# A two-block kernel (bidirectional Mamba, then a mixture of experts): the routed experts' outputs are scaled by ScalarE on their way out of PSUM and added up by GpSimd, in place of VectorE

## The chip, the cores and the metric

The program runs on one core of a Trainium2 chip. The metric is the time of one execution on the device, in microseconds (us). Engines are named as in the profile: PE is TensorE (PEld its weight loads), DVE is VectorE, ACT is ScalarE, POOL is GpSimd, SP is SyncE, which issues the transfers.

## The reference, cut to what matters

There are 16 sequences of 512 tokens with 128 channels. Each goes through a normalisation, a Mamba block run forwards and backwards (256 inner channels, 16 states), a second normalisation, and a mixture of eight routed experts, of which a token uses two, plus one shared expert:

```
gate_out = x @ gate_w
top_v, top_i = jax.lax.top_k(gate_out, TOP_K)            # TOP_K = 2 of 8
w = softmax over the chosen two, 0 elsewhere
swiglu(x, w1, w2, w3) = h * sigmoid(h) * (x @ w2) @ w3,  h = x @ w1
out = sum over e of swiglu(x, ew1[e], ew2[e], ew3[e]) * w[..., e]
out = out + swiglu(x, sw1, sw2, sw3)
```

All is float32. Every expert is computed for every token, and the weight `w` is zero where the token did not choose it. The change touches only the sum over experts.

## The kernel before, in words

All engines run programs written out by hand, in the same order of work: `passes` calls `body(b, ...)` for b = 0 to 16. Body b holds the scan of sequence b (both directions) beside the mixture of experts of sequence b-1, the preparation of the backward direction of b, and that of the forward direction of b+1. Body 0 has no experts, body 15 prepares nothing for a next sequence, body 16 has only the experts of sequence 15 (below: the tail). Bodies 1 to 14 are alike.

A body has 32 **slots**, one for each scan step: slots 0 to 15 are the 16 states forwards, 16 to 31 backwards. Within a slot s:

- DVE scans two halves of 128x512 (L792, reads `psA` in PSUM and `bt`), then multiplies each by `cb` into `g` (L802). Between the two L802 it makes `pf` (L891) from ScalarE's `tf` and the expert's first product in PSUM bank F0. After them it does its side work: `zs` or `u` (L832), `yg` (L850, shown as `acc`), statistics (L808), and in some slots the expert sum (L905).
- ACT first evicts an expert's two products as `tf` and `gf` (L686, L689: `expert_turns`), then writes the two `exp` tiles that the next slot's scans need (L604: `exps`, each waits for the `g` of the same half), then its side work: `xn`/`z` (L657), `th` (L622, L625), `ab`/`xb` (L641 to L645), and in slots 9 and 28 `ln1p` (L652, L653), which loads another activation table, computes, and loads the old one again.
- POOL first makes `bt` for the next slot (L430), then side work (`dt` L474, `v` L479, `hx`, `wg`, the output `fx` and `osb` L484, L487 in slot 0), then `act` (L520) from `pf` and `gf`.
- PE adds the previous slot's `g` into `psY` (L996), then its expert work and preparation: the down projection of an expert into PSUM bank F2 (L1122), convolutions (L1012), `skip_and_turn` (L1033, L1035), and last the two up projections into F0 and F1 (L1083, L1086).

The down projection of expert e takes two slots (`down_at`: part 0 and part 1). For e = 1 to 8 the part 1 slots are 15, 17, 19, 21, 24, 26, 28 and 30. Expert 0 is the shared one; ACT copies it to `facc` (L707). There is one bank F2, so PE waits at part 0 of expert e until that of e-1 has been read; before, that is a wait on `facc_s`. `expert_sum` does four instructions on DVE for each routed expert, one for each 128 tokens: `facc = F2 * wts + facc`, with the weight as a per-partition operand, in the part 1 slot. GpSimd's `output` reads `facc` at the end. Every wait is a semaphore count; an engine runs its own list strictly in order.

Of the kernel before, what the change touches and what calls it, by code (L numbers as in the profile page):

```python
# [70 lines left out]
def adaln_mamba_moe(nc, t, out):  # L71
# [3 lines left out]
    with ctx:  # L75
# [6 lines left out]
        def sem(name):  # L82
            return ctx.enter_context(nc.semaphore(name))
# [105 lines left out]
        pf = sb("pf", [P, 2, T])  # L189
        act = sb("act", [P, 3, 2, T])  # L190
        facc = sb("facc", [P, NT, D])
        osb = sb("osb", [P, NT, D])
# [67 lines left out]
        pf_s = sem("pf_s")  # L260
        act_s = sem("act_s")
        facc_s = sem("facc_s")
        gw_s = sem("gw_s")
# [143 lines left out]
        def _(pool):  # L407
# [73 lines left out]
            def output(fb):  # L481

                pool.wait_ge(facc_s, NX * NT * fb + NX * NT)
                g.tensor_tensor(fx[:, :, :], facc[:, :, :], over_tiles(modF[:, :]), ALU.mult).then_inc(o_s, 1)  # L484
                pool.wait_ge(o_s, 2 * fb + 1)
                wait(pool, out_d, 16 * fb)
                g.tensor_tensor(osb[:, :, :], fx[:, :, :], x2[:, :, :], ALU.add).then_inc(o_s, 1)  # L487

            def expert_weights(fb):
# [9 lines left out]
                pool.wait_ge(wts_s, q + 2)  # L499
                wait(pool, facc_s, NX * NT * fb)  # L500
                g.tensor_tensor(wts[:, :, :], hotw[:, 0, :, :], hotw[:, 1, :, :], ALU.add).then_inc(wts_s, 1)

            def ffn_side(fb, slot):
# [10 lines left out]
                if k is not None:  # L514
# [5 lines left out]
                    g.tensor_tensor(act[:, k // 2 % 3, k % 2, :], pf[:, k % 2, :], gf[:, k % 3, :], ALU.mult)\  # L520
                        .then_inc(act_s, 1)

            def gated_weights(b):
# [26 lines left out]
            def body(b, scan, ffn, last):  # L550
                for slot in range(STEPS):
# [12 lines left out]
                    if ffn:  # L564
                        ffn_side(b - 1, slot)

            passes(pool, body)
# [4 lines left out]
        def _(act_e):  # L572
# [118 lines left out]
            def ffn_side(fb, slot):  # L691
# [12 lines left out]
                if down_at(slot) == (0, 1):  # L704
                    act_e.wait_ge(F2_full, (DOWN + NE) * fb + DOWN + 1)
                    wait(act_e, o_s, 2 * fb)
                    s.activation(facc[:, :, :], F2[:, :], ACT.Copy).then_inc(F2_free, 1)  # L707

            for slot in range(STEPS):
# [38 lines left out]
        def _(dve):  # L748
# [144 lines left out]

            def expert_sum(fb, slot):

                down = down_at(slot)
                if down and down[0] and down[1]:
                    e = down[0]
                    dve.wait_ge(F2_full, (DOWN + NE) * fb + DOWN + e + 1)
                    if e == 1:  # L900
                        dve.wait_ge(F2_free, (DOWN + 1) * fb + DOWN + 1)
                        dve.wait_ge(wts_s, 3 * fb + 3)
                    wait(dve, facc_s, NX * NT * fb + NT * (e - 1))
                    for i in range(NT):
                        w.scalar_tensor_tensor(facc[:, i, :], F2[:, i * D:i * D + D],  # L905
                                               wts[:, i, ORDER[e]:ORDER[e] + 1], facc[:, i, :],
                                               ALU.mult, ALU.add).then_inc(facc_s, 1)

            def ffn_side(fb, slot):
# [28 lines left out]
            def body(b, scan_, ffn, last):  # L938
                for slot in range(STEPS):
# [10 lines left out]
                    if ffn:  # L950
                        ffn_side(b - 1, slot)
                        expert_sum(b - 1, slot)
                    if scan_ and slot - POST_F_SLOT in (0, 1):
# [6 lines left out]
        def _(pe):  # L960
# [95 lines left out]
            def ffn_side(fb, slot):  # L1056
                free = (DOWN + 1) * fb
                if slot - POSTB_SLOT in (0, 1):
                    half = slot - POSTB_SLOT
                    if half == 0:  # L1060
                        pe.wait_ge(acc_s, 4 * fb + 4)
                        wait(pe, facc_s, NX * NT * fb)
                    else:
# [25 lines left out]
            def ffn_late(fb, slot):  # L1089
# [22 lines left out]
                if down:  # L1112
                    e, part = down
                    if part == 0:
# [3 lines left out]
                        else:  # L1118
                            pe.wait_ge(facc_s, NX * NT * fb + NT * (e - 1))
                    for i in (2 * part, 2 * part + 1):  # L1120
# [57 lines left out]
```

## Time and profile before

| | |
|---|---|
| median of 3 runs | 2525.33 us (2525.15 to 2533.57) |
| the profiled execution | 2529.96 us |
| its span | 2528.1 us |
| busy in the span | DVE 91%, PE 82%, POOL 77%, ACT 60% |
| bodies 1 to 14 | 149.0 us each |
| body 15 | 144 us |
| body 16, the tail | 86 us |

The profiled execution lies 4.6 us over the median, 0.2%. Busy shares are means over the whole span. Since each engine works through its own list in order, the place to read is a slot: which engine had to wait in it, and for whom. The list of instructions in order of time shows that: its columns are the start (us from the span's start), how long, the engine, the line, the operation with its output and inputs, how many were merged into the row, and in brackets how long the engine had been idle before and who released it. Successive instructions of an engine overlap a little, so a row's duration is more than the distance to the next one's start.

### The profile page before, as it was taken

What the parts mean: (1) busy time and instruction counts of PE and PEld (TensorE: products, weight loads), DVE (VectorE), ACT (ScalarE), POOL (GpSimd) and SP (SyncE); (2) the same over time, 40 slices, a digit from 0 to 9 for tenths busy, and PEclk for the clock granted to TensorE, in tenths of its full rate; (3) what the DMA queues carried; (4) which work ended last, traced back from release to release, by engine and by line L of the source; (5) the groups of instructions that cost most, each with busy time, mean ns of one, the idle gap of its engine ahead of it and who ended that gap; (6) DMA issues with size and microseconds to landing.
All of it is one profiled execution on the core that took longest, in us unless ns stands there. A gap on an engine that the chain in (4) does not pass through costs nothing. (4 is left out here: it accounts for less than half of the span.)

```text
span 2528.1 us, 31606 instructions
## 1 busy us (share of the span) xinstructions
PE 2078.9 (82%) x9893; PEld 1307.9 (52%) x9893; DVE 2298.2 (91%) x3843; ACT 1505.8 (60%) x2468; POOL 1936.1 (77%) x1259
## 2 busy tenths in 40 slices
PE   3667887989888797988879888888988878898868
PEld 1344554545555465555546555454655545565545
DVE  1699999999999999999999999999999999999963
ACT  2545656665666666556666665666666576666633
POOL 1576888878788787878878788787878888787844
PEclk9678999989999998999999899898999999899989
DMA  3334243333433333342333333333333433333310
GB/s 85 127 126 143 100 131 119 110 131 109 137 105 125 122 111 131 110 139 101 118 131 110 131 109 131 118 110 125 118 131 109 137 112 111 132 112 130 109 55 5
DMA packets 112107, 291.16 MB, mean 115 GB/s; under 512 B 18260, under 2 KB 44724, under 8 KB 111940
## 3 DMA queue, kind: packets, MB, share of 16 engines
q1 hardware_dynamic: 111940, 289.15, 33.6%
q8 instruction: 78, 1.28, 0.2%
q14 instruction: 89, 0.73, 0.1%
HBM read 282.77 MB, written 6.34 MB: 114 GB/s over the span
## 5 line engine op out<-in xcount | busy, mean ns | idle before, releaser
L430 POOL TENSOR_TENSOR bt<-v,bb 128x1024 f32<-128x1024 f32 x512 | 1208.6, 2361 | 175.2 <-DVE psA L792 173.2
L792 DVE TENSOR_TENSOR_SCAN psA<-psA,bt 128x512 f32<-128x512 f32 x1024 | 1196.2, 1214 | 62.6 <-ACT psA L604 60.6
L604 ACT ACTIVATE psA<-dt,aneg 128x512 f32<-128x512 f32 x1024 | 687.8, 688 | 732.3 <-DVE g L802 731.8
L996 PEld LDWEIGHTS psY<-ident,g 128*128 128x128 f32 x4096 | 504.1, 149 | 428.1 <-DVE g L802 212.2
L996 PE MATMUL psY<-ident,g 128*128 128x128 f32 x4096 | 601.5, 290 | 129.2 <-DVE g L802 128.0
L802 DVE TENSOR_TENSOR g<-psA,cb 128x512 f32<-128x512 f32 x1024 | 673.4, 677 | 0.0
L520 POOL TENSOR_TENSOR act<-pf,gf 128x512 f32<-128x512 f32 x288 | 366.2, 1271 | 290.8 <-DVE pf L891 269.1
L1083 PE MATMUL F<-h2T,w 128*128 128x512 f32 x576 | 329.5, 656 | 100.4 <-DVE pf L891 99.5
L1122 PE MATMUL F<-w,act 128*128 128x128 f32 x2304 | 308.8, 277 | 14.5 <-DVE facc L905 8.3
L1086 PE MATMUL F<-h2T,w 128*128 128x512 f32 x576 | 314.0, 629 | 0.0
L1122 PEld LDWEIGHTS F<-w,act 128*128 128x128 f32 x2304 | 282.3, 193 | 29.5 <-POOL act L520 25.5
L1012 PE MATMUL psP<-xnT,wcT 128*128 128x512 f32 x512 | 255.2, 623 | 4.4 <-DVE u L832 2.1
L891 DVE SCALAR_TENSOR_TENSOR pf<-tf,F 128x512 f32<-128x512 f32 x288 | 195.0, 677 | 51.0 <-ACT tf L686 48.3
L686 ACT ACTIVATE tf<-F 128x512 f32<-128x512 f32 x288 | 170.2, 591 | 75.3 <-PE F L1083 74.9
L1083 PEld LDWEIGHTS F<-h2T,w 128*128 128x128 f32 x576 | 95.1, 197 | 212.1 <-DVE pf L891 163.7
L689 ACT ACTIVATE gf<-F 128x512 f32<-128x512 f32 x288 | 172.7, 600 | 51.6 <-PE F L1086 51.0
L1028 PE MATMUL psP<-xnT,wzT 128*128 128x512 f32 x128 | 96.0, 842 | 123.0 <-DVE zs L832 121.7
L1086 PEld LDWEIGHTS F<-h2T,w 128*128 128x128 f32 x576 | 115.8, 201 | 150.1 <-issue 149.5
L905 DVE SCALAR_TENSOR_TENSOR facc<-F,wts,facc 128x128 f32<-128x128 f32 x512 | 143.3, 343 | 5.2 <-PE F L1122 5.2
L1012 PEld LDWEIGHTS psP<-xnT,wcT 128*128 128x128 f32 x512 | 92.8, 202 | 76.7 <-issue 67.6
L625 ACT ACTIVATE th<-psP 128x512 f32<-128x512 f32 x128 | 75.7, 592 | 52.9 <-PE psP L1028 50.8
L474 POOL TENSOR_TENSOR dt<-xb,ab 128x1024 f32<-128x1024 f32 x32 | 75.3, 2355 | 33.9 <-ACT ab L652 33.8
(130 smaller groups left out, 1700.1 us busy)
## 6 DMA issues: line engine op xcount, KB each, us to landing
bb<-bc_rows SPq DMA_DIRECT2D x256, 512.0 KB, 3.7
cb<-bc_rows SPq DMA_DIRECT2D x256, 512.0 KB, 3.7
x<-in_L_attn_x SPq DMA_DIRECT2D x16, 256.0 KB, 4.3
out_x<-osb SPq DMA_DIRECT2D x16, 256.0 KB, 4.5
modA<-mod_table SPq DMA_DIRECT2D x16, 192.0 KB, 4.4
w<-in_L_ffn_ew SPq DMA_DIRECT2D x2, 1024.0 KB
bc_rows<-xd SPq DMA_DIRECT2D x32, 64.0 KB, 3.2
modG<-mod_table SPq DMA_DIRECT2D x16, 64.0 KB, 4.0
```

The costliest lines, as they stand in the source:

```text
L430: g.tensor_tensor(bt[:, n % 2, :, :], v[d][:, :, :], bb[:, n // 2 % 2, n % 2, :].unsqueeze(1).broadcast_to([P, NH, T]), ALU.mult).then_inc ...
L520: g.tensor_tensor(act[:, k // 2 % 3, k % 2, :], pf[:, k % 2, :], gf[:, k % 3, :], ALU.mult)\
L604: s.activation(psA[:, half * T:half * T + T], dt_[d][:, half, :], ACT.Exp, scale=aneg[d][:, half, n:n + 1]).then_inc(a_s, 1)
L689: s.activation(gf[:, k % 3, :], F1[:, :], ACT.Copy).then_inc(F1_free, 1)
L792: w.tensor_tensor_scan(ah, ah, bt[:, n % 2, half, :][:, order], 0.0, ALU.mult, ALU.add)\
L802: w.tensor_tensor(g_[:, n % 2, half, :], psA[:, half * T:half * T + T], cb[:, n // 2 % 2, n % 2, :], ALU.mult).then_inc(g_s, 1)
L891: w.scalar_tensor_tensor(pf[:, k % 2, :], tf[:, k % 2, :], 1.0, F0[:, :], ALU.add, ALU.mult).then_inc(pf_s, 1)
L996: last = m.matmul(psY[:, half * T + i * P:half * T + i * P + P], g_[:, n % 2, half, i * P:i * P + P], ident[:, :], is_transpose=True, star ...
L1012: last = m.matmul(psP[:, :], wcT[d][:, half, j, :], xnT[:, lo:lo + T], start=(j == 0), stop=(j == TAPS - 1))
L1083: m.matmul(F0[:, :], w1[:, x_, half * P:half * P + P], h2T[:, :], start=True, stop=True)\
L1086: m.matmul(F1[:, :], w2[:, x_, half * P:half * P + P], h2T[:, :], start=True, stop=True)\
L1122: last = m.matmul(F2[:, i * D:i * D + D], act[:, e % 3, half, i * P:i * P + P], w3[:, ORDER[e], half, :], start=(half == 0), stop=(half == 1))
```

## The change

A new buffer `fe` (two tiles of 128x4x128) stands between PSUM and the sum. In the part 1 slot of each routed expert ACT now reads F2 in four instructions with the weight as its per-partition scale and writes `fe`, behind that slot's `exps` and ahead of its side work. One slot later POOL adds the whole tile, `facc = facc + fe`, in one instruction behind `act`. DVE's `expert_sum` is gone. PE's wait before the next down projection moves from the sum (`facc_s`) to the eviction (`fe_s`).

```
+        fe = sb("fe", [P, 2, NT, D])

   POOL, output(fb):
-                pool.wait_ge(facc_s, NX * NT * fb + NX * NT)
+                pool.wait_ge(facc_s, NX * fb + NX)
   POOL, expert_weights(fb):
-                wait(pool, facc_s, NX * NT * fb)
+                wait(pool, fe_s, NX * NT * fb)

   POOL:
+            def expert_sum(fb, slot):
+                down = down_at(slot)
+                if down and down[0] and down[1]:
+                    e = down[0]
+                    pool.wait_ge(fe_s, NX * NT * fb + NT * e)
+                    if e == 1:
+                        pool.wait_ge(F2_free, (DOWN + 1) * fb + DOWN + 1)
+                    wait(pool, facc_s, NX * fb + e - 1)
+                    g.tensor_tensor(facc[:, :, :], facc[:, :, :], fe[:, e % 2, :, :], ALU.add).then_inc(facc_s, 1)
                     if ffn:
                         ffn_side(b - 1, slot)
+                        expert_sum(b - 1, slot - 1)

   ACT, at the end of ffn_side(fb, slot):
+                down = down_at(slot)
+                if down and down[0] and down[1]:
+                    e = down[0]
+                    act_e.wait_ge(F2_full, (DOWN + NE) * fb + DOWN + e + 1)
+                    if e == 1:
+                        act_e.wait_ge(wts_s, 3 * fb + 3)
+                    wait(act_e, facc_s, NX * fb + e - 2)
+                    for i in range(NT):
+                        s.activation(fe[:, e % 2, i, :], F2[:, i * D:i * D + D], ACT.Copy,
+                                     scale=wts[:, i, ORDER[e]:ORDER[e] + 1]).then_inc(fe_s, 1)

   DVE:
-            def expert_sum(fb, slot):
-                down = down_at(slot)
-                if down and down[0] and down[1]:
-                    ...
-                    for i in range(NT):
-                        w.scalar_tensor_tensor(facc[:, i, :], F2[:, i * D:i * D + D],
-                                               wts[:, i, ORDER[e]:ORDER[e] + 1], facc[:, i, :],
-                                               ALU.mult, ALU.add).then_inc(facc_s, 1)
                         ffn_side(b - 1, slot)
-                        expert_sum(b - 1, slot)

   PE, ffn_side and ffn_late:
-                        wait(pe, facc_s, NX * NT * fb)
+                        wait(pe, fe_s, NX * NT * fb)
-                            pe.wait_ge(facc_s, NX * NT * fb + NT * (e - 1))
+                            pe.wait_ge(fe_s, NX * NT * fb + NT * (e - 1))
```

The order of instructions on ACT, slots 15 and 16, before:

```order
L604 ACTIVATE psA<-dt,aneg 128x512 x2
L657 ACTIVATE xn<-z,stat,rstd 128x128 x4
L612 ACTIVATE acc<-psY 128x512 x2
L686 ACTIVATE tf<-F 128x512
L689 ACTIVATE gf<-F 128x512
```

and in the changed kernel, where the same functions stand 14 lines further down:

```order
L618 ACTIVATE psA<-dt,aneg 128x512 x2
L730 ACTIVATE fe<-F,wts 128x128 x4
L671 ACTIVATE xn<-z,stat,rstd 128x128 x4
L626 ACTIVATE acc<-psY 128x512 x2
L700 ACTIVATE tf<-F 128x512
L703 ACTIVATE gf<-F 128x512
```

The four `fe` stand between the exponentials and three kinds of work that precede the next `tf`.

ACT, slots 26 (from its two exponentials) to 29, in the changed kernel; before, the rows are the same without the two of L730:

```order
L618 ACTIVATE psA<-dt,aneg 128x512 x2
L730 ACTIVATE fe<-F,wts 128x128 x4
L655 ACTIVATE ab<-psP,bdt 128x512
L656 ACTIVATE xb<-psP,bdt 128x512
L659 ACTIVATE ab<-ab 128x512
...
L666 ACT_TABLE_LOAD
L666 ACTIVATE ab<-ab 128x1024
L667 ACT_TABLE_LOAD
L730 ACTIVATE fe<-F,wts 128x128 x4
L618 ACTIVATE psA<-dt,aneg 128x512 x2
```

In slot 26 the eviction stands ahead of `ab`, in slot 28 behind the second table load and directly ahead of the exponentials for slot 30.

POOL, from slot 29's `bt` to slot 1's, before:

```order
L430 TENSOR_TENSOR bt<-v,bb 128x1024
L474 TENSOR_TENSOR dt<-xb,ab 128x1024
L430 TENSOR_TENSOR bt<-v,bb 128x1024
L479 TENSOR_TENSOR v<-u,dt 128x1024
L430 TENSOR_TENSOR bt<-v,bb 128x1024 x2
L484 TENSOR_TENSOR fx<-facc,modF 128x512
L487 TENSOR_TENSOR osb<-fx,x 128x512
```

and in the changed kernel:

```order
L432 TENSOR_TENSOR bt<-v,bb 128x1024
L476 TENSOR_TENSOR dt<-xb,ab 128x1024
L534 TENSOR_TENSOR facc<-facc,fe 128x512
L432 TENSOR_TENSOR bt<-v,bb 128x1024
L481 TENSOR_TENSOR v<-u,dt 128x1024
L432 TENSOR_TENSOR bt<-v,bb 128x1024
L534 TENSOR_TENSOR facc<-facc,fe 128x512
L432 TENSOR_TENSOR bt<-v,bb 128x1024
L486 TENSOR_TENSOR fx<-facc,modF 128x512
L489 TENSOR_TENSOR osb<-fx,x 128x512
```

Two of the eight sums fall in here, one ahead of slot 30's `bt` and one ahead of slot 0's.

## Rows read from the trace of the kernel before

**Rows 1.** The page, busy time of each engine over the whole span.

```profile
PE 2078.9 (82%) x9893; PEld 1307.9 (52%) x9893; DVE 2298.2 (91%) x3843; ACT 1505.8 (60%) x2468; POOL 1936.1 (77%) x1259
```

**Rows 2.** One body: length, busy of PE, PEld, DVE, ACT, POOL, granted clock, DMA.

```profile
1007.60:1156.60 149.00, 127.37 (x616) 80.79 (x616) 142.93 (x239) 93.41 (x154) 120.91 (x79) 0.93 0.35 120
```

**Rows 3.** In order of time, DVE, slots 19 to 21.

```profile
1051.61 1.12 DVE L905 SCALAR_TENSOR_TENSOR facc<-F,wts,facc 128x128 f32<-128x128 f32 x4
1052.64 2.33 DVE L792 TENSOR_TENSOR_SCAN psA<-psA,bt 128x512 f32<-128x512 f32 x2
1056.67 2.34 DVE L792 TENSOR_TENSOR_SCAN psA<-psA,bt 128x512 f32<-128x512 f32 x2
```

**Rows 4.** Groups by line: busy, mean ns of one, idle before them and its releaser.

```profile
L604 ACT ACTIVATE psA<-dt,aneg 128x512 f32<-128x512 f32 x1024 | 687.8, 688 | 732.3 <-DVE g L802 731.8
...
L657 ACT ACTIVATE zF<-x,statF,rstdF 128x128 f32<-128x128 f32 x64 | 26.1, 479 | 16.9 <-POOL statF L442 16.9
```

**Rows 5.** In order of time, slots 15 and 16.

```profile
1032.16 1.63 ACT L657 ACTIVATE xn<-z,stat,rstd 128x128 f32<-128x128 f32 x4
1034.82 0.60 ACT L686 ACTIVATE tf<-F 128x512 f32<-128x512 f32 x1
1035.45 0.69 DVE L891 SCALAR_TENSOR_TENSOR pf<-tf,F 128x512 f32<-128x512 f32 x1
1036.20 1.12 PE L1083 MATMUL F<-h2T,w 128*128 128x512 f32 x2 [1.06 <-DVE pf L891]
```

**Rows 6.** PE by stretch, slots 17 to 22: length, busy (instructions), granted clock, DMA.

```profile
1041.00:1066.00 25.00, 25.00 (x131) 1.00 0.33 111
```

**Rows 7.** In order of time, slots 17 to 21.

```profile
1040.64 1.05 PE L1035 MATMUL psP<-ident,acc 128*128 128x128 f32 x8
1041.74 0.69 DVE L850 TENSOR_TENSOR acc<-psP,zs 128x512 f32<-128x512 f32 x1
...
1055.46 1.88 PE L1012 MATMUL psP<-xnT,wcT 128*128 128x512 f32 x4
...
1057.41 0.64 ACT L622 ACTIVATE psP<-psP,convb 128x512 f32<-128x512 f32 x1
...
1058.58 0.59 ACT L686 ACTIVATE tf<-F 128x512 f32<-128x512 f32 x1
...
1059.50 0.67 DVE L891 SCALAR_TENSOR_TENSOR pf<-tf,F 128x512 f32<-128x512 f32 x1
```

**Rows 8.** In order of time, slot 27.

```profile
1086.22 0.59 ACT L686 ACTIVATE tf<-F 128x512 f32<-128x512 f32 x1
1087.69 0.67 DVE L891 SCALAR_TENSOR_TENSOR pf<-tf,F 128x512 f32<-128x512 f32 x1
```

**Rows 9.** In order of time, slots 29 and 30.

```profile
1097.61 1.30 ACT L604 ACTIVATE psA<-dt,aneg 128x512 f32<-128x512 f32 x2
1098.40 2.35 DVE L792 TENSOR_TENSOR_SCAN psA<-psA,bt 128x512 f32<-128x512 f32 x2 [0.74 <-ACT psA L604]
```

**Rows 10.** PE by stretch, as Rows 6, slots 30 to 0, then 8 and 9.

```profile
1099.00:1101.00 2.00, 0.27 (x3) 1.00 0.56 215
1102.00:1107.00 5.00, 4.33 (x13) 0.50 0.29 105
...
1144.00:1145.00 1.00, 0.50 (x2) 1.00 0.46 172
...
1146.00:1149.00 3.00, 3.00 (x5) 0.50 0.01 3
```

**Rows 11.** In order of time, POOL, slots 29 to 2.

```profile
1096.44 2.36 POOL L474 TENSOR_TENSOR dt<-xb,ab 128x1024 f32<-128x1024 f32 x1 [0.17 <-ACT ab L652]
1110.78 2.35 POOL L430 TENSOR_TENSOR bt<-v,bb 128x1024 f32<-128x1024 f32 x1
1115.28 2.34 DVE L792 TENSOR_TENSOR_SCAN psA<-psA,bt 128x512 f32<-128x512 f32 x2
```

**Rows 12.** In order of time, the end of the tail.

```profile
2522.73 1.26 POOL L484 TENSOR_TENSOR fx<-facc,modF 128x512 f32<-128x512 f32 x1 [3.44 <-DVE facc L905]
```

More of the change, by code:

```diff
@@ L261, in adaln_mamba_moe @@
         act_s = sem("act_s")
+        fe_s = sem("fe_s")
         facc_s = sem("facc_s")
@@ L892, in expert_silu @@
                                            ALU.add, ALU.mult).then_inc(pf_s, 1)
-            def expert_sum(fb, slot):
-                down = down_at(slot)
-                if down and down[0] and down[1]:
[L898 to L903, printed above, removed]
-                    for i in range(NT):
-                        w.scalar_tensor_tensor(facc[:, i, :], F2[:, i * D:i * D + D],
-                                               wts[:, i, ORDER[e]:ORDER[e] + 1], facc[:, i, :],
-                                               ALU.mult, ALU.add).then_inc(facc_s, 1)
             def ffn_side(fb, slot):
```

## The prediction

> **What bounds the kernel now.** I read the busy shares first, then the stretches, then single slots in order of time. DVE is busy for 91% of the span [rows 1] and for 142.9 of the 149.0 us of a body [rows 2], PE for 127, POOL for 121, ACT for 93. So DVE sets the pace by the mean. But a body is a mixture of slots with different limits. In a slot with an expert sum DVE starts the next scan 1.03 us later than it could: the sum starts at 1051.61, the scan behind it at 1052.64; the slot after it, without a sum, is 4.03 us long [rows 3]. Eight sums make 8.24 us a body, and over bodies 1 to 15 that is 123.6 us, 4.9% of the time: what a reader of the shares alone would expect back. The order of time shows who is next in line.
>
> **What is added on ACT.** A row for this eviction does not exist. An `exp` with a per-partition scale takes 0.688 us [rows 4], a `tanh` of as many elements with a constant 0.59 [rows 8]: 0.10 us for the operand. The 128x128 normalisation, which has two such operands, takes 0.479 us [rows 4]; less one of them, 0.38. Four of them take 1.63 us, so neighbours overlap by (4 x 0.479 - 1.63)/3 = 0.095 us [rows 5]. The eviction then holds ACT for 4 x (0.382 - 0.095) = 1.15 us. Bounds: 0.76 us if it cost two operands less than the normalisation, 1.54 if it cost as much as scale and bias. I take 1.15, since both parts come from rows of the same shape or operand. It is as long as what it replaces on DVE, but it lands on an engine that DVE waits for: ACT's list is `tf`, `gf`, two exponentials, eviction, side work, and the next `tf` is behind it all. In most part 1 slots ACT has 1.3 us or more to spare before the next `tf` is wanted, and the eviction costs nothing. In three it does not.
>
> **Slots 15 and 16.** ACT works without a pause from `xn` to `tf`, and `pf` starts at 1035.45, 0.03 us after `tf` ends [rows 5]. The eviction ahead of `xn` moves both by 1.15 us. The sum's 1.03 us go, and `pf` of slot 16 is 1.15 later than now. PE's next up projection waits for that `pf`, already after 1.06 us of idleness [rows 5].
>
> **Slots 17 to 21.** PE is busy in all 25 us of this stretch, at the full clock (2.4 GHz) [rows 6]. DVE's `yg` follows PE's last transpose directly (1040.64 + 1.05 = 1041.69, starts 1041.74), and so does ACT's `u` preparation (1055.46 + 1.88 = 1057.34, starts 1057.41), on which the `pf` at 1059.50 depends [rows 7]. Since PE has started 1.15 later and has no gap to make it good, slots 17 and 18 stay 1.15 late whatever DVE saves. In 19 one sum comes back, but PE's convolution then holds `pf` of slot 21: about 0.8 late (1.15, less the 0.33 us between the end of `tf`, 1058.58 + 0.59, and 1059.50 [rows 7]). The sum of slot 21 comes off: 0.2 early. Three of four sums have paid for one eviction and for PE.
>
> **Slots 24 to 28.** The sums of 24 and 26 come off in full: 2.2 us early. In slot 26 the eviction stands ahead of `ab`, and the next `tf` in the trace ends at 1086.81, 0.88 before its `pf` [rows 8]. With exponentials 1.2 early and an eviction of 1.15 it ends at about the same time, 1086.8, so `pf` of slot 27 starts there: 0.9 early, and 1.3 us are lost. Slot 28 adds its sum: 1.9 early.
>
> **Slots 28 to 30.** ACT's logarithm with its two table loads already makes DVE wait 0.74 us for the exponentials of slot 30 [rows 9]. The eviction of slot 28 comes between them: 0.9 early - 1.15 = 0.25 late. The sum of slot 30 makes it 0.8 early. PE's down projection of slot 29 now waits for that eviction until about 1097.9, and the `z` projection, ACT's `th` and ACT's next exponentials stand behind it. PE idles some 5 us. The clock fell to 0.5 (1.2 GHz) in this trace after PE had been busy for 0.27 of 2 us, a little later in the same slots, and stayed there from 1102 to 1107 [rows 10]. I expect the fall some 3 us sooner, over exactly this work: two 0.9 us pieces at half speed put `th` at 1102.5 and slot 31 half a microsecond later. **A body is then 0.8 - 0.5 = 0.3 us shorter** (0.27 unrounded).
>
> **POOL.** It adds one 128x512 sum for each expert, 1.26 us by the like product [rows 12], 1.23 with overlap: 9.8 us a body on 120.9. Two fall into the stretch where POOL works on without a pause from 1096.44 to 1110.78 + 2.35 = 1113.13, ahead of the scan of slot 2 at 1115.28 [rows 11]. With them, and a start 0.9 earlier, it ends at 1114.8. That is 0.2 us before a scan that is 0.3 early; a body that is more than 0.5 early is held here. In slots 24 to 28 POOL needs 2 x (2.36 + 1.26) + 1.26 = 8.5 us, less overlaps, for a pair of slots (a `bt` is as large as the `dt` of [rows 11], an `act` as the product of [rows 12]) against DVE's 2 x 4.03 = 8.06 [rows 3], and DVE waits for ACT there anyhow. `expert_weights` and the output wait for nothing new that is late.
>
> **Body 15 and the tail.** Body 15 prepares nothing, so slots 26 to 30 are free of ACT's trouble; slots 15 to 18 are bound by PE as above. Six sums come off (6.2 us), less about 1.2 where POOL's pair is longer: 5 us. In the tail the eviction stands ahead of `tf`, which the next `pf` and PE follow: some 0.2 us for each of seven experts, then after the last expert 1.26 us of POOL more ahead of `fx` [rows 12]: 2.7 us lost. Together 2.3 us gained.
>
> **The clock in slot 16.** PE's wait before the up projection grows from 1.06 to some 2.2 us. With 1.06 the clock stayed; but it was at 0.5 from 1146 on after PE had been busy for only 0.50 of the us from 1144 [rows 10]. So it may fall here too. In those bodies PE, which sets the pace in 17 to 21, does its work at 1.2 GHz for about as long as the 3 us row: 1.7 us late, and nothing behind it makes that good, since the later evictions take the slack that was left. Such a body is 1.4 us longer than now. The phase of the falls changes from body to body, so I take five bodies of 14. The Trainium skill ("TensorE: Matmul & The Clock Gate", HAM oscillation) counts only longer pauses of PE as dangerous; by that rule slot 16 keeps its clock and the time would be that of the first rival. The row at 1146 speaks against it.
>
> **The sum.** 9 x 0.3 - 5 x 1.4 + 2.3 = -2.0, with unrounded terms -2.4: a span of 2530.5 against 2528.1, and on the median 2525.3 + 2.4 = 2528 us.
>
> **The rivals.** (1) The clock holds in slot 16: 14 x 0.27 + 2.3 = 6 us gained, 2519. For it: PE's full clock through all of slots 15 to 22 now. (2) It falls in every body: 14 x 1.4 - 2.3 = 17.5 us lost, 2543. That is the slower side: a wait turned into half speed on the engine that binds the next five slots; it decides from about nine bodies on. For it: 2.2 us without PE is more than what preceded the fall at 1146. (3) The low clock costs nothing in 29 to 31 either, or the eviction is 0.76 us: up to 0.5 us a body until POOL holds, 9 us, 2516; with POOL's hold absent 0.8 to 1.6 a body, 2512 to 2500. (4) DVE really is the bound and all sums come off: 2525 - 124 + 3 = 2404. Against it: all four waits of [rows 5, 7, 8, 9]. (5) The eviction is 1.54 us: 0.4 more at two places, 14 x 0.8 = 11 us on the forecast, 2539.
>
> **Chances.** Forecast 0.30, rival 1 0.20, rival 2 0.18, rival 5 0.08 (most of it within 0.5% unless the clock adds to it), rival 3 0.20 (16 parts of it beyond 0.5%, where POOL doesn't hold either), rival 4 0.04. The measurement can tell about 0.5% (12.6 us) from no change: faster 0.16 + 0.04 = 0.20, slower 0.18 and 0.05 of rival 5 = 0.23, same the remaining 0.57. The range reaches to rival 2 and to the nearer part of 3, and leaves out rival 4, the far part of 3 and what goes beyond 2: 2508 to 2545.
>
> **What would show it.** In the profile after: DVE busy some 132 us less, ACT some 150 us more, POOL some 160 more, and the idle time before `pf` (from `tf`), before `yg` (from PE) and before the scans (from the exponentials) grown by nearly as much as DVE saved. Bodies of 148.7 or 150.4 us, by whether the clock falls at slot 16. The eviction at 0.38 us each. It is wrong if `pf` of slot 16 or 27 does not wait, if PE pauses in slots 17 to 20, or if DVE's waits name POOL's `bt`.

## The result: 0.8% slower

The changed kernel takes 2547.23 us in the median of 6 runs (2541.91 to 2553.92), the kernel before 2526.64 in 6 runs beside it (2525.15 to 2533.57): a ratio of 1.0076, 95% interval 1.0056 to 1.0096. The forecast was 2528 us, with a range of 2508 to 2545, so the direction of its second rival came, not that of the forecast. The profiled execution took 2547.57 us, its span is 2545.7.

**Busy time moved as forecast.** The page of the changed kernel, which answers [rows 1]:

```profile
PE 2084.2 (82%) x9893; PEld 1324.4 (52%) x9893; DVE 2175.0 (85%) x3331; ACT 1630.9 (64%) x2980; POOL 2089.7 (82%) x1387
```

DVE has 123 us less, ACT 125 and POOL 154 more (forecast 132, 150 and 160). The two new groups, columns as in [rows 4]:

```profile
L730 ACT ACTIVATE fe<-F,wts 128x128 f32<-128x128 f32 x512 | 144.7, 364 | 13.1 <-PE F L1130 12.5
...
L534 POOL TENSOR_TENSOR facc<-facc,fe 128x512 f32<-128x512 f32 x128 | 163.2, 1275 | 4.3 <-ACT fe L730 4.2
```

One eviction takes 364 ns where 382 was worked out, POOL's sum 1.275 us where 1.26 was taken. The Trainium skill ("ScalarE: Activation LUTs", What ACT_TABLE_LOAD costs) has the terms of an `ACTIVATE`; an estimate from them for 128 elements with one pointer operand is 186 + 0.833 x 128 + 93 = 386 ns. The trace has 22 ns less.

**And the time went into waits.** Waits of DVE, the whole span: who, for whom, us in total, times, longest. After:

```profile
DVE pf L915 <- ACT tf L700: 102.5, 76, 7.0
DVE psA L816 <- ACT psA L618: 85.6, 109, 2.6
DVE acc L874 <- PE psP L1043: 36.2, 31, 2.7
DVE psA L816 <- POOL bt L432: 28.3, 40, 1.7
```

and before:

```profile
DVE pf L891 <- ACT tf L686: 48.3, 33, 5.1
DVE psA L792 <- ACT psA L604: 60.6, 116, 2.0
...
DVE acc L850 <- PE psP L1035: 8.7, 16, 1.0
```

The first three have grown by 54, 25 and 27.5 us. The fourth, for POOL's `bt`, was 1.7 us in all before and is one that the prediction said would show it wrong. Together the four have grown by 133 us: that is where DVE's 123 us went, and most of the 17.6 us by which the span is longer.

**Two kinds of bodies.** Two bodies from the scan of slot 15 to the end, columns as in [rows 2]: without and with a fall of PE's clock in slots 16 and 17.

```profile
1178.87:1258.92 80.05, 71.42 (x368) 47.18 (x366) 70.73 (x88) 59.25 (x116) 74.71 (x46) 0.98 0.34 112
1328.50:1410.35 81.85, 74.01 (x368) 49.15 (x366) 70.73 (x89) 59.22 (x116) 74.51 (x45) 0.94 0.32 108
```

In the kernel before this stretch is 80.11 us in every one of the 14 bodies (to 0.02), however long the body is as a whole: that varies, from 147.24 to 149.78, only with what happens in slots 0 to 14, where the clock falls several times in changing places. So it is the measure for all that follows. In the changed kernel it is 79.9 to 80.2 in 6 bodies and 81.8 to 81.9 in 8. DVE is busy for 7.7 us less of it, and a body without the fall is no more than 0.1 shorter.

### The profile page after: what moved, and what is told of

Read it like the earlier page. It is cut to its first block and busy times, and to the rows that moved or that the text cites. A ratio compares the mean times of both kernels' runs of the same rounds, so it can differ in the third digit from the quotient of the medians.

```text
span 2545.7 us, 31846 instructions
## 1 busy us (share of the span) xinstructions
PE 2084.2 (82%) x9893; PEld 1324.4 (52%) x9893; DVE 2175.0 (85%) x3331; ACT 1630.9 (64%) x2980; POOL 2089.7 (82%) x1387
## 5 line engine op out<-in xcount | busy, mean ns | idle before, releaser
L1004 PE MATMUL psY<-ident,g 128*128 128x128 f32 x4096 | 587.2, 287 | 124.3 <-DVE g L826 123.4
L1091 PE MATMUL F<-h2T,w 128*128 128x512 f32 x576 | 340.1, 675 | 96.1 <-DVE pf L915 96.1
L1130 PE MATMUL F<-w,act 128*128 128x128 f32 x2304 | 327.1, 288 | 75.1 <-ACT fe L730 69.6
L1130 PEld LDWEIGHTS F<-w,act 128*128 128x128 f32 x2304 | 299.8, 203 | 90.1 <-issue 73.3
L1094 PE MATMUL F<-h2T,w 128*128 128x512 f32 x576 | 326.6, 651 | 0.0
L534 POOL TENSOR_TENSOR facc<-facc,fe 128x512 f32<-128x512 f32 x128 | 163.2, 1275 | 4.3 <-ACT fe L730 4.2
L730 ACT ACTIVATE fe<-F,wts 128x128 f32<-128x128 f32 x512 | 144.7, 364 | 13.1 <-PE F L1130 12.5
```

The costliest lines, as they stand in the source:

```text
L1004: last = m.matmul(psY[:, half * T + i * P:half * T + i * P + P], g_[:, n % 2, half, i * P:i * P + P], ident[:, :], is_transpose=True, star ...
L1091: m.matmul(F0[:, :], w1[:, x_, half * P:half * P + P], h2T[:, :], start=True, stop=True)\
L1094: m.matmul(F1[:, :], w2[:, x_, half * P:half * P + P], h2T[:, :], start=True, stop=True)\
L1130: last = m.matmul(F2[:, i * D:i * D + D], act[:, e % 3, half, i * P:i * P + P], w3[:, ORDER[e], half, :], start=(half == 0), stop=(half == 1))
```

## Slot by slot

**Slot 16.** In order of time, a body with the fall:

```profile
1333.27 1.13 ACT L730 ACTIVATE fe<-F,wts 128x128 f32<-128x128 f32 x4
1334.28 1.65 ACT L671 ACTIVATE xn<-z,stat,rstd 128x128 f32<-128x128 f32 x4
...
1336.77 0.61 ACT L700 ACTIVATE tf<-F 128x512 f32<-128x512 f32 x1
...
1337.41 0.69 DVE L915 SCALAR_TENSOR_TENSOR pf<-tf,F 128x512 f32<-128x512 f32 x1 [1.97 <-ACT tf L700]
...
1338.15 1.50 PE L1091 MATMUL F<-h2T,w 128*128 128x512 f32 x2 [1.53 <-DVE pf L915]
...
1339.45 1.91 PE L1094 MATMUL F<-h2T,w 128*128 128x512 f32 x2
...
1345.38 0.69 DVE L874 TENSOR_TENSOR acc<-psP,zs 128x512 f32<-128x512 f32 x1 [2.66 <-PE psP L1043]
```

and one body earlier, without:

```profile
1188.52 1.12 PE L1091 MATMUL F<-h2T,w 128*128 128x512 f32 x2 [1.52 <-DVE pf L915]
...
1189.48 1.02 PE L1094 MATMUL F<-h2T,w 128*128 128x512 f32 x2
...
1194.06 0.69 DVE L874 TENSOR_TENSOR acc<-psP,zs 128x512 f32<-128x512 f32 x1 [0.97 <-PE psP L1043]
```

The chain is as forecast: `fe`, `xn`, `tf`, then `pf`, which now waits 1.97 us, then PE, then `yg` (shown as `acc`) behind PE. The eviction holds ACT for 1334.28 - 1333.27 = 1.01 us. The scans from slot 17 on are 0.84 later than in the kernel before, not 1.15: 0.14 of the eviction's estimate was too much, and the other 0.17 is taken up between the start of `xn` and that of `tf`, 2.49 us here and 2.66 before [rows 5]. PE's pause is 1.52 us, not 2.2, since the transposes of `xn` come later too. In the first body the up projections take 1.50 and 1.91 us, in the second 1.12 and 1.02. PE by stretch (length, busy, granted clock, DMA), from slot 16's scan and 2 us to slot 18's scan, a body with and one without:

```profile
433.90:445.37 11.47, 9.79 (x48) 0.85 0.32 110
584.26:594.03 9.77, 8.09 (x48) 1.00 0.25 94
```

The same 48 matmuls take 1.70 us longer, part of them at 1.2 GHz. 8 of the 14 rows of this view have 0.85, 6 have 1.00; before, all have 1.00.

**Slots 21 to 27: POOL.** POOL and DVE's scans, in order of time, slots 20 to 24, and the scan of slot 27:

```profile
1207.52 1.28 POOL L522 TENSOR_TENSOR act<-pf,gf 128x512 f32<-128x512 f32 x1 [0.43 <-DVE pf L915]
...
1208.76 1.27 POOL L534 TENSOR_TENSOR facc<-facc,fe 128x512 f32<-128x512 f32 x1
...
1212.31 1.28 POOL L464 TENSOR_TENSOR hx<-z,modA 128x512 f32<-128x512 f32 x1
...
1218.33 1.27 POOL L534 TENSOR_TENSOR facc<-facc,fe 128x512 f32<-128x512 f32 x1
1219.56 2.36 POOL L432 TENSOR_TENSOR bt<-v,bb 128x1024 f32<-128x1024 f32 x1
1221.87 1.29 POOL L467 TENSOR_TENSOR hx<-hx,x 128x512 f32<-128x512 f32 x1
1221.95 2.35 DVE L816 TENSOR_TENSOR_SCAN psA<-psA,bt 128x512 f32<-128x512 f32 x2 [1.09 <-POOL bt L432]
...
1235.20 2.35 DVE L816 TENSOR_TENSOR_SCAN psA<-psA,bt 128x512 f32<-128x512 f32 x2 [0.48 <-POOL bt L432]
```

POOL works from 1207.52 on without a pause, and the scan of slot 24 waits 1.09 us for its `bt`, that of slot 27 0.48. The prediction had asked for this in slots 24 to 28 alone and in `bt`, `act` and `sum`: it left out the two `hx` of slots 21 and 23, the `wg` of slot 25, and the sums of slots 20 and 22. Without the length of the sums (e8 below) neither wait is there; the same scan of slot 24 in the same body:

```profile
1215.24 2.35 DVE L816 TENSOR_TENSOR_SCAN psA<-psA,bt 128x512 f32<-128x512 f32 x2 [0.23 <-ACT psA L618]
```

**Slots 28 to 30.** As forecast, and worse. In order of time:

```profile
1248.63 1.14 ACT L730 ACTIVATE fe<-F,wts 128x128 f32<-128x128 f32 x4
1249.65 1.32 ACT L618 ACTIVATE psA<-dt,aneg 128x512 f32<-128x512 f32 x2
1249.92 1.94 PE L1130 MATMUL F<-w,act 128*128 128x128 f32 x8 [4.79 <-ACT fe L730]
1250.46 2.35 DVE L816 TENSOR_TENSOR_SCAN psA<-psA,bt 128x512 f32<-128x512 f32 x2 [2.62 <-ACT psA L618]
1251.66 1.91 PE L1036 MATMUL psP<-xnT,wzT 128*128 128x512 f32 x2
...
1253.61 0.60 ACT L639 ACTIVATE th<-psP 128x512 f32<-128x512 f32 x1 [2.64 <-PE psP L1036]
```

The eviction stands ahead of the exponentials, PE has been idle for 4.79 us and works off two groups at half speed, and the scan of slot 30 waits 2.62 us where [rows 9] had 0.74. That all came as worked out, in place and in kind.

The shifts of the scans against the kernel before, counted from slot 15, in a body without the fall in slot 16 (us, late is +):

| scan of slot | 17 | 20 | 22 | 24 | 25 | 27 | 28 | 29 | 30 | end |
|---|---|---|---|---|---|---|---|---|---|---|
| forecast | 1.15 | 0.1 | -0.2 | -0.2 | -1.2 | -2.2 | -0.9 | -1.9 | 0.25 | -0.3 |
| trace | 0.84 | -0.19 | -0.49 | 0.36 | -0.67 | -1.15 | -0.47 | -1.32 | 0.57 | -0.07 |

Up to slot 22 the trace is ahead of the forecast by the 0.3 us of slot 16. At 24 POOL takes 0.85 and at 27 half a microsecond more, and from there on it is behind.

**The tail.** It is 6.5 us longer from the last scan on. PE in order of time, the output gating of the last sequence, the first down projection and that of expert 1:

```profile
2464.88 5.58 PE L1109 MATMUL F<-wg,acc 128*128 128x128 f32 x32 [0.83 <-issue]
...
2488.49 3.27 PE L1130 MATMUL F<-w,act 128*128 128x128 f32 x16 [2.08 <-POOL act L522]
...
2498.81 1.05 PE L1130 MATMUL F<-w,act 128*128 128x128 f32 x8
```

The last row starts 48.1 us after the last scan; in the kernel before it is 43.5, with 3.81 and 2.05 us in place of 5.58 and 3.27. So 4.6 us are clock, before the first eviction was made at all. They are not the change's own: the trace of e4, with the same tail, doesn't have them, and that of e9 does. The seven experts behind it lose 0.6 to the evictions, and the end loses 1.3 to POOL's last sum.

## Experiments

One table for all of them: the median and the ratio to the kernel before in the same comparison, and from the traces the mean length of the two parts of bodies 1 to 14. The second part, from the scan of slot 15 on, is given without and with the fall in slots 16 and 17. The counts of falls are those of one execution of each kernel, the profiled one; the median is over all.

| | median us | ratio (95%) | slots 0 to 14 | slot 15 to end | bodies with fall |
|---|---|---|---|---|---|
| before | 2526.4 to 2529.4 | 1 | 68.85 | 80.11 | 0 |
| changed | 2547.23 | 1.0076 (1.0056 to 1.0096) | 68.96 | 80.02, 81.84 | 8 |
| e1 no sum | 2475.11 | 0.9803 (0.9787 to 0.9820) | 68.62 | 76.90 | 0 |
| e2 ACT's load | 2590.27 | 1.0265 (1.0244 to 1.0286) | 69.19 | 82.59, 84.28 | 13 |
| e3 short POOL sum | 2535.51 | 1.0038 (1.0024 to 1.0052) | 69.18 | 78.91, 80.85 | 13 |
| e4 PE filled | 2531.61 | 1.0024 (1.0012 to 1.0035) | 68.84 | 80.08 | 0 |
| e5 experts 3, 5, 8 | 2496.45 | 0.9872 (0.9855 to 0.9888) | 68.68 | 77.98 | 0 |
| e6 experts 4, 5, 8 | 2493.91 | 0.9870 (0.9848 to 0.9893) | 68.63 | 77.89 | 0 |
| e7 experts 3, 4, 5, 8 | 2489.61 | 0.9851 (0.9831 to 0.9871) | 68.47 | 77.78 | 0 |
| e8 both e3 and e4 | 2513.53 | 0.9939 (0.9922 to 0.9955) | 68.81 | 79.16 | 0 |
| e9 expert 1 alone | 2533.72 | 1.0020 (1.0008 to 1.0032) | 68.19 | 80.97, 82.66 | 2 |
| e10 all but expert 1 | 2520.78 | 0.9969 (0.9956 to 0.9982) | 68.97 | 79.17 | 0 |
| e11 before, PE filled | 2528.35 | 1.0000 (0.9990 to 1.0010) | 68.65 | 80.12 | 0 |
| e12 experts 4, 5, 6, 8 | 2498.55 | 0.9889 (0.9872 to 0.9907) | 69.01 | 77.89 | 0 |

**e1, without the sums.** From the kernel before:

```
-                        expert_sum(b - 1, slot)
```

> The kernel before without DVE's expert sums, and with nothing in their place (the routed experts' sum is left out; PE and POOL no longer wait for it). This takes away what the change takes from DVE and adds nothing to ACT, POOL or PE. Theory A (mine: slots have different limits, and DVE is not the last to be waited for in all of the eight): some 4 to 5 us a body come off, since ACT, PE and the exponentials are next in line in slots 16, 27 and 30; about 2460 us. Theory B (DVE is the bound everywhere): all 1.03 us of 8 sums in 15 bodies, 124 us, come off: 2403. If it gives less than 30 us, DVE's sums were hidden anyway, and the change could not have won in any form.

Measured: 2475.11 us, 51 less. DVE is not the bound in all eight slots, theory A; of 8.24 us of sums 3.2 come off in a body, less than I had said. Slots 16, 17 and 21, where ACT's `tf` and PE are waited for, take 1.0, 1.0 and 0.7 us, and slots 27 to 30 another 2.3, even when nothing is added to ACT. By this, 50 us are about the most that such a change can win.

**e2, ACT's load alone.** From the kernel before; the sums on DVE stay:

```
+                    for i in range(NT):
+                        s.activation(fe[:, e % 2, i, :], h2T[:, i * D:i * D + D], ACT.Copy,
+                                     scale=wts[:, i, ORDER[e]:ORDER[e] + 1]).then_inc(fe_s, 1)
```

> The kernel before, unchanged, plus ACT's four scaled 128x128 copies in each part 1 slot, at the place where the changed kernel has them; they read h2T and nothing uses what they write. DVE keeps its sums, POOL adds nothing. It measures what ACT's added work costs by itself. Theory A (ACT's eviction moves pf in slots 16 and 27 and the exponentials in slots 28 to 30): about 1 us later at slot 16, 0.1 to 0.2 at slot 27 (the cover of 0.88 us is nearly enough), 1 at slot 30, 2 to 3 us a body: 30 to 45 us slower, 2555 to 2570. Theory C (POOL's sums are what costs; ACT has room): within 5 us of the kernel before.

Measured: 2590.27 us, 64 more, where 30 to 45 were forecast. The places are those named: the scans are 0.98 later from slot 17 on, 0.33 from slot 28, 1.17 from slot 30, 2.5 in a body, which makes 35 us. Most of the rest is the clock: it fell in 13 of 14 bodies, 1.69 us each, 22 us; slots 0 to 14 have 5 us more. PE by stretch, slots 16 and 17, the body without a fall and the next:

```profile
286.16:294.88 8.72, 7.21 (x40) 1.00 0.24 78
437.88:448.46 10.58, 8.76 (x39) 0.84 0.27 100
```

**e3, POOL's sum short.** From the changed kernel:

```
-                    g.tensor_tensor(facc[:, :, :], facc[:, :, :], fe[:, e % 2, :, :], ALU.add).then_inc(facc_s, 1)
+                    g.tensor_tensor(facc[:, :, 0:1], facc[:, :, 0:1], fe[:, e % 2, :, 0:1], ALU.add).then_inc(facc_s, 1)
```

> The changed kernel with POOL's sum on one column of each 128 (most of the sum is left out), so that POOL has room and all waits stay. Theory A (the falls of PE's clock at slots 16 and 17 and ACT's length are the main losses; POOL costs what the trace shows at slots 24 and 27, 1.1 and 0.5 us, of which part is found again at the next wait for ACT): 0.5 to 1.3 us a body, 8 to 20 us faster than the changed kernel, 2527 to 2540, and falls in about 8 of 14 bodies remain. Theory C (POOL is what costs): all 20 us and more come back and the kernel beats the one before, under 2515.

Measured: 2535.51 us, 12 less than the changed kernel, inside the range of theory A. But the sum takes 210 ns here, the one body without a fall is 1.1 us shorter in its second part, and the fall now comes in 13 bodies and not in 8:

```profile
L534 POOL TENSOR_TENSOR facc<-facc,fe 128x4 f32<-128x4 f32 x128 | 26.9, 210 | 7.5 <-ACT fe L730 6.7
```

So one gain was partly eaten by the other cause. Bodies 3 to 12 of this run are all between 150.09 and 150.17 us long: they are nearly equal, and the clock falls at the same places in each.

**e4, PE filled.** From the changed kernel, the four transposes of `xn` in slot 16 three times over:

```
-                        for i in range(NT):
+                        for i in range(3 * NT):
+                            i = i % NT
                             last = m.transpose(psP[:, i * P:i * P + P], xn[:, i, :], ident[:, :])
```

> The changed kernel with PE's four transposes of xn in slot 16 done three times, the same values into the same place, so that PE is busy in part of the pause ahead of the first up projection; everything else is the same and the output too. Theory A (the 8 of 14 bodies that take 150.4 to 151.6 us in place of 147.6 to 149.2 do so for the granted clock falling to 1.2 GHz in slots 16 and 17): the fall goes from these slots, 8 x 1.7 = 14 us come back, about 2533. Rival D (the falls go with something else, and the long bodies have another cause): the time stays within 4 us of 2547, or grows, while the rows show the clock at 2.4 GHz.

Measured: 2531.61 us (9 runs), 15.6 less than the changed kernel, with more work on PE. PE's pause ahead of the first up projection is 0.65 us in place of 1.52, and slots 16 and 17 have the full clock in all 14 bodies. In order of time, then PE by stretch:

```profile
1187.51 1.12 PE L1092 MATMUL F<-h2T,w 128*128 128x512 f32 x2 [0.65 <-DVE pf L915]
...
438.35:448.11 9.76, 8.96 (x56) 1.00 0.29 95
...
1183.89:1193.66 9.77, 8.97 (x56) 1.00 0.32 96
```

By the traces, the falls give 14.6 us. The tail is 4.6 us shorter too (its first two groups take 3.81 and 2.05 us again), though nothing was filled there: that is where the clock's falls happen to come. Against it, the first scan of body 1 is 4.5 us later. This is a price of the filling: it is 3.6 us later in e11 and 3.9 in e8 too, and in no kernel without the filling. Most of it, 2.4 to 3.2 us in these three, lies ahead of the first scan of all, where the same transposes prepare the first sequence with nothing beside them.

**e11, the control.** The same three lines in the kernel before.

> Control: the kernel before with xn's transposes three times in slot 16. The clock is at 2.4 GHz there anyway. Theory A: nothing to win: the same as before, or 1 to 2 us slower for body 0, where the extra transposes lie open. If it is more than 5 us faster, the extra transposes help in another way than by slots 16 and 17, and the 14 us of the filled kernel are not the price of those falls.

Measured: 2528.35 us, ratio 1.000 (0.999 to 1.001). The second part of a body is 80.12 us, as before (80.11): where the clock is full anyway, the filling wins nothing in slots 16 and 17, and what e4 won there is the price of the falls. The equal total is less telling than it looks. In the trace the start loses 3.6 us to the filling, and slots 0 to 14 (2.8 us) and the tail (1.9) happen to be shorter.

**e8, both.** The edits of e3 and e4 together.

> The changed kernel with both edits: xn's transposes three times in slot 16, and POOL's sum on one column of each 128 (most of the sum is left out). The run with the short sum alone was 12 us faster than the changed kernel, but the clock fell in slots 16 and 17 in 13 bodies in place of 8. If the two causes add: 8 x 1.7 = 14 us for the clock and 12 + 5 x 1.7 = 20 us for POOL, 34 in all, 2513. If POOL's cost is only the 12 us that were measured: 2521 or more. If the two are one and the same loss: 2531.

Measured: 2513.53 us; theory A had 2513. Clock and POOL are two causes and they add. POOL's sums cost 18 us (2531.6 to 2513.5): by the traces 0.92 us in the second part of each body, 13 in all, 2.5 in body 15 and 2.7 in the tail. The 12 us of e3 are about this sum less five more falls (9 us), with 4.6 of clock less in the tail and 3 us more in slots 0 to 14.

**e9, expert 1 alone.** `ON_ACT` names the experts that go through ACT and POOL; the others keep DVE's four instructions as before. The split kernels differ from each other in this one line:

```
+ON_ACT = (1,)
```

> Only expert 1 (slot 15) goes through ACT and POOL; the other seven stay with DVE as before. One part of the change alone. Theory A (this eviction alone starts PE late in slot 16 and brings the fall of its clock): the scan of slot 16 comes 1.03 us earlier, that of slot 17 some 0.84 later than before, for good: 14 x 0.84 = 12 us, and 1.7 us more in each body in which the clock falls; with 8 such bodies 14 us, with all of them 24: 2552 to 2562, while it should be 2538 without any fall. Rival C (POOL's sums and the slots from 24 on make the loss): within 5 us of the kernel before.

Measured: 2533.72 us (10 runs), 5 more than before. The delay of the scans is as said, 0.86 us in every body (80.97 against 80.11). But the clock fell in 2 bodies, and slots 0 to 14 are 0.66 us shorter on the mean, since the falls there come in other places: 14 x 0.86 + 2 x 1.69 - 14 x 0.66 = 6 us, and this is what bodies 1 to 14 of the trace have. (Its whole span is 11 us longer than that of before, with 4.6 of clock in the tail; the profiled execution is 7 us over the median.) Theory A is right on the wait and wrong on its price. More telling is how alike a body with the fall and one without are. In order of time, body 1, which has it:

```profile
291.42 0.69 DVE L930 SCALAR_TENSOR_TENSOR pf<-tf,F 128x512 f32<-128x512 f32 x1 [1.97 <-ACT tf L713]
...
292.17 1.39 PE L1130 MATMUL F<-h2T,w 128*128 128x512 f32 x2 [1.52 <-DVE pf L930]
...
293.35 1.91 PE L1133 MATMUL F<-h2T,w 128*128 128x512 f32 x2
```

and body 2, which has not:

```profile
442.45 0.69 DVE L930 SCALAR_TENSOR_TENSOR pf<-tf,F 128x512 f32<-128x512 f32 x1 [1.97 <-ACT tf L713]
...
443.19 1.13 PE L1130 MATMUL F<-h2T,w 128*128 128x512 f32 x2 [1.52 <-DVE pf L930]
...
444.15 1.02 PE L1133 MATMUL F<-h2T,w 128*128 128x512 f32 x2
```

The pause is 1.52 us in both, and the work of the 12 us ahead of it is the same. Bodies 11 and 13 are alike for 30 us back, with pauses of 4.34, 1.43, 1.45, 0.28 and 1.52 us in both, and only the first has the fall. The length doesn't decide alone either. In the kernel before, PE keeps its clock behind the 1.06 us of [rows 5], and in slot 8 it runs at half of it behind 1.15, with 1.78 us for what takes 1.12 there:

```profile
1145.64 1.78 PE L1083 MATMUL F<-h2T,w 128*128 128x512 f32 x2 [1.15 <-DVE pf L891]
```

So the longer pause makes the fall in slot 16 possible. What is left to decide on it is where in time the pause comes, but no run moved that alone: it is argued, not shown.

**e10, all but expert 1.** `ON_ACT = (2, 3, 4, 5, 6, 7, 8)`.

> The changed kernel with expert 1 alone given back to DVE (slot 15); the other seven go through ACT and POOL. Theory A: PE starts slot 16 as before, the clock falls in no body in slots 16 and 17 (8 x 1.7 = 14 us back), and the 0.84 us of delay of every body go too (12 us); 1.2 us of POOL's work less on top: 26 us under the changed kernel or a little more, 2517 to 2521, which is faster than before. Rival F (all eight evictions cost alike): an eighth of the loss, 2545.

Measured: 2520.78 us, 26 under the changed kernel, in the range of theory A, and faster than before (ratio 0.9969, 0.9956 to 0.9982). The second part of a body is 79.17: 0.94 less than before, where e9 had 0.86 more. Their sum, -0.08, is that of the changed kernel without falls. One expert of eight undid what seven had won.

**e5 to e7 and e12, splits.** Sums move only where the run without sums had kept what they gave.

> Experts 3, 5 and 8 (slots 19, 24, 30) go through ACT and POOL as in the changed kernel, the other five stay with DVE as before; the output is the full one. The run without any sum showed which of DVE's sums are worth something: the scans behind those of experts 3, 5 and 8 came 1.03 us earlier and stayed so, that behind expert 4 0.3, while what those of 1, 2 and 7 gave was lost at the next wait for PE or ACT, and all before slot 30 is cut back to 2.2 there. Theory A (a sum is worth moving where DVE is waited for and ACT and POOL have room; the losses came from the evictions in slots 15, 26 and 28 and from POOL's sums one after the other): 3 us a body, no fall of PE's clock in slots 16 and 17, no wait for POOL's bt in slot 24; 14 x 3 + 3 in body 15 - 2 in the tail = 43 us less than before, about 2483. Rival E (each eviction or sum on ACT and POOL costs about what DVE saves, wherever it stands): the same as before within 10 us.

> The same split with expert 4 (slot 21) in place of 3. Its sum stood in a slot where the run without sums gained 0.3 us only, since PE binds there. Theory A: 2.3 to 2.4 us a body, about 10 us slower than the split 3, 5, 8: 2493. Rival E (it doesn't matter which slots): equal to the split 3, 5, 8.

> The same split with experts 3, 4, 5 and 8. DVE has one sum less to make. Theory A: what the sums up to slot 29 give is cut back to 2.2 us at slot 30, which 3 and 5 nearly reach, so the fourth brings at most 0.2 us a body, and POOL's sums of 3 and 4 stand in its full stretch ahead of slot 24: the same as the split 3, 5, 8 within 5 us, about 2483. Rival B (DVE is the bound): 1 us a body less, 2470.

> The split 4, 5, 8 with expert 6 (slot 26) added. Its eviction stands ahead of ab and of the next tf. Theory A: DVE's 1.03 us come off at slot 27, of which the wait of pf for tf takes a part at once, and the rest is cut back to 2.2 us ahead of slot 30: 0 to 0.2 us a body, 2490 to 2494, the same as the split 3, 4, 5, 8. Rival B (DVE is the bound there): 1 us a body, 2479.

Measured: 2496.45, 2493.91, 2489.61 and 2498.55 us. All four beat both kernels, by 1.1 to 1.5% of the one before; 3, 4, 5 and 8 has the lowest median, 40 us under it, though its interval overlaps those of the first two. Two statements on them fell. The first split was to give 3 us a body and gave 2.1, and the second was to be 10 us behind it and is level. I had read e1 by the shifts of its scans, where expert 4's slot seemed to keep 0.3 us. It keeps all of its 1.03, but the scan of slot 22 first loses 0.73 of expert 3's gain, since `pf` waits for a `tf` that is behind PE's convolution. The wait in the split 3, 5, 8:

```profile
1338.45 0.69 DVE L930 SCALAR_TENSOR_TENSOR pf<-tf,F 128x512 f32<-128x512 f32 x1 [0.64 <-ACT tf L713]
```

A cumulated shift is a sum of two changes and names neither. That the fourth expert adds little came as said, and in e7 POOL's `bt` is the reason: with the sums of 3 and 4 in its full stretch the scan of slot 24 waits for it again,

```profile
1345.25 2.35 DVE L831 TENSOR_TENSOR_SCAN psA<-psA,bt 128x512 f32<-128x512 f32 x2 [1.07 <-POOL bt L445]
```

where 0.85 us of the two sums are lost. In e6, with the sum of 4 alone there, 0.67 of it is lost at the same place. Expert 6 adds nothing to the second part of a body (77.89 with and without), as said, but half of its gain goes at the scan of slot 27, which now waits 0.47 us for POOL's `bt`. That e12 is 5 us slower than e6 lies in slots 0 to 14, 0.38 us longer a body. Of that, 0.31 is lost up to the scan of slot 2, which waits 0.36 us for POOL's `bt` on the mean, and 0.05 in e6.

## Why the prediction was wrong

By the traces the span grew by 17.6 us where 2.4 was forecast. The difference of 15.2, by the terms of the sum:

| | forecast | trace | difference |
|---|---|---|---|
| up to body 1 | 0 | -1.1 | -1.1 |
| bodies without falls | 14 x -0.27 = -3.8 | 14 x (-0.09 + 0.11) = 0.2 | 4.0 |
| falls in slots 16 and 17 | 5 x 1.7 = 8.4 | 8 x 1.82 = 14.6 | 6.2 |
| body 15 and tail | -2.3 | 3.9 | 6.2 |

(-0.09 is the second part of a body, 80.02 against 80.11, 0.11 the first.) Another 4 us of the miss in the median lie in the base: the profiled execution of before was 4.6 us above its median, that of after 0.3, so "the difference of the spans on the median" moved by that much.

Two steps of the prediction failed: the number of falls, taken as 5 and 8 in the trace, and POOL, taken at nothing in bodies 1 to 14 where its sums cost 13 us. The table shows only 4 us for the second, since the other terms of a body came out 0.68 us better than forecast and hide the rest. Of its last row 4.6 us are where the clock fell in that one execution.

- **The number of falls.** The mechanism was right: the eviction of slot 15 makes PE wait, the clock falls, 1.7 us are lost, nothing behind makes it good. The size was right by luck: the 3 us row at half the clock that it went by gives 1.5, the runs show 1.69 to 1.70, and 1.82 to the end of the body in the changed kernel. "The phase of the falls changes from body to body, so I take five bodies of 14" was no measurement. It was 8 here, 13 in e2 and e3, 2 in e9, with pauses of 1.50 to 1.53 us in all of them, and none in the ten other kernels, whose pauses there are 1.06 us or less. The 2.2 us that it forecast for the pause were 1.52. Rival 2, with every body, was nearer in the time than the forecast (2543), but it had the cause wrong in part: no POOL and six falls too many. The Trainium skill's rule ("TensorE: Matmul & The Clock Gate", HAM oscillation), by which only longer pauses are dangerous, doesn't hold for slot 16 here. Its next section (A second HAM failure mode), on many short pauses between groups of matmuls, is nearer to these rows.
- **POOL.** Its sums cost 18 us (e8 against e4), 13 in bodies 1 to 14, where the forecast had nothing, and 5 in body 15 and the tail, where it had 2.5. The prediction counted POOL's work from slot 24 on, of `bt`, `act` and sum, and left out `hx`, `wg` and what came before slot 24. It looked for POOL's hold ahead of slot 2 and set aside slots 24 to 28; it is there that the trace has 0.85 and about half a microsecond. It said that DVE's waits for `bt` would show it wrong, and they do (28.3 us). Without POOL's sums a body would have been better than forecast: e8 has 0.95 us less in the second part, the forecast 0.27, half of the difference from slot 16 alone.
- **ACT's eviction** was 1.15 us in the sum and 1.01 in the trace, `pf` of slot 16 is 0.84 later and not 1.15. The sign and the place were right in slots 16, 28 and 30, and in slot 27 as e8 shows it, where 1.24 us go (1.3 forecast). Slots 17 and 18 stay late as said, and in slot 21 PE takes back 0.73 us of a sum, as said.
- **Slots 28 to 30.** That the exponentials behind the logarithm take back what came before was right, and e1 shows that they do it without any eviction too.
- **Body 15 and the tail.** Body 15 gained 2.6 us up to its last scan, not 5. The difference is POOL: in e8 it gains 5.5. The tail lost 6.5 where 2.7 was said. In e4, which has the same evictions and sums there, it lost 1.9, as in the rows above, where 0.6 are ACT's and 1.3 POOL's. The term of ACT was 1.4, more than twice what it cost; the other 4.6 are clock.
- **Rival 4** (DVE as the bound) is refuted by e1, which takes DVE's sums away and gets 51 of 124 us. **Rival 1**, the kernel without falls, was put at 2519. The nearest run is e4 with 2531.6, which also carries the filling's 4 us at the start; the other 8 or 9 are less than the 13 us that POOL's sums take in the bodies.

What stays open is what decides in which body the clock falls. e4 and e10, with pauses of 0.65 and 1.06 us and no fall in slot 16, show that the longer pause is needed there, and e9 that it isn't enough. It wasn't tried to shift the pause in small steps against the falls of the slots before.

## What to carry to other kernels

Before work is moved off the busiest engine, take it away altogether and run that (e1): here 51 of 124 us were to be had, and the traces of that run and of one with the load alone on its new engine (e2) say in which slots. Then move it only where the gain is kept and the new engine is not itself waited for: four of eight sums gave 40 us, all eight lost 20. And where a matmul engine sets the pace with short pauses in it, count a longer pause not as its own length but with the clock's fall behind it, in every body as the bad end of the range; filling the pause with work that nobody needs got 15.6 us back in all, after a price of some 4 us where the filling stood alone.

## What the runs showed of the hardware

- PE's granted clock falls behind a pause of 1.52 us in one body and holds behind the same pause in the next (e9), so the same program has bodies of two lengths, 1.7 us apart, and a small change elsewhere can alter how many there are: 2, 8 or 13 of 14. Behind a pause of 1.06 us or less in the same slot it held in all 14 bodies of ten kernels, while in slot 8 of the kernel before it fell behind 1.15.
- An edit elsewhere moves the falls of other stretches too: slots 0 to 14, which no edit touched in their work but for POOL's first slots, took from 67.1 to 70.0 us, and on the mean of a kernel 68.19 (e9) to 69.19 (e2). That is up to 14 us in the time, more than most of the terms of the sum.
- A scaled 128x128 copy on ACT takes 364 ns from PSUM, and in e2 387 ns from SBUF (L717 of that kernel), for the same output.
